# Residual rows kept in SBUF over four stages, zero fills moved, three stages rewritten as skewed pipelines

## The reference

```
h = relu(windowed product of x with filt * W_k + b_k)      # token:      [64, 248, 64]
h = h + attention(layernorm(h))                            # attention:  8 heads of 8, patch and position scores mixed
h = h + ffn(layernorm(h))                                  # feed-forward: only the 123 rows of largest router score,
                                                           #   gelu(x w1 + b1) w2 + b2, times the score
h = h + recurrent(layernorm(h))                            # key, table, recurrent: q, k, v and gates, then a
                                                           #   sequential update of two small MLPs over 248 steps
h = h + experts(layernorm(h))                              # 8 experts, two of them chosen a row
```

## Time and profile before

| | us |
|---|---|
| median of three runs | 10781.3 (10769.8 to 10793.7) |
| profiled execution, span from first to last instruction (its own time) | 10794.5 |
| TensorE busy | 9005.6 (83%) |
| VectorE busy | 4911.9 (46%) |
| ScalarE busy | 2097.8 (19%) |
| GpSimd busy | 227.2 (2%) |

### The profile page before, as it was taken

One profiled execution on the slowest core, in us unless ns is written; L12 is line 12 of the kernel. 1 busy time (PEld: TensorE's weight loads), 2 busy tenths in 40 slices (PEclk: granted clock), 3 DMA queues, 4 the chain that ended last, 5 costly groups with the idle time before them and its releaser, 6 DMA issues. The chain is left out here.

```text
span 10794.5 us, 373142 instructions
## 1 busy us (share of the span) xinstructions
PE 9005.6 (83%) x152370; PEld 5786.4 (54%) x152370; DVE 4911.9 (46%) x13031; ACT 2097.8 (19%) x4839; POOL 227.2 (2%) x184
## 2 busy tenths in 40 slices
PE   6799953424699999999999999999999999967777
PEld 2466631122466676666666766667667666642222
DVE  3444435446634444444344444443443444445555
ACT  0233321221111111111111111111111111113343
POOL 0000000001100000000000000000000000000000
PEclk8799975557899999999999999999999999988888
DMA  2000001425311121211111211222222222200000
GB/s 61 8 11 11 11 22 39 137 41 105 85 30 55 54 57 53 56 55 55 56 55 52 57 54 56 79 74 82 69 75 81 73 76 77 61 19 12 12 9 11
DMA packets 961796, 563.30 MB, mean 52 GB/s; under 512 B 376334, under 2 KB 956694, under 8 KB 959766
## 3 DMA queue, kind: packets, MB, share of 16 engines
q1 hardware_dynamic: 947990, 544.62, 18.7%
q0 software_dynamic: 13312, 12.57, 0.6%
HBM read 331.63 MB, written 188.08 MB: 48 GB/s over the span
## 5 line engine op out<-in xcount | busy, mean ns | idle before, releaser
L2387 PE MATMUL bank<-mv,hdiag 128*32 128x144 f32 x63744 | 2052.5, 286 | 11.2 <-DVE hdiag L2580 9.5
L2387 PEld LDWEIGHTS bank<-mv,hdiag 128*32 128x32 f32 x63744 | 1933.5, 110 | 85.8 <-DVE hdiag L2580 12.5
L2440 PE MATMUL bank<-mvt,ydiag 128*32 128x256 f32 x31872 | 1942.6, 381 | 0.0
L2440 PEld LDWEIGHTS bank<-mvt,ydiag 128*32 128x32 f32 x31872 | 1038.1, 110 | 568.8 <-issue 1.0
L2289 PE MATMUL bank<-yth,r_ident 128*128 128x512 f32 x896 | 507.9, 678 | 119.3 <-ACT mv L2232 58.8
L2243 ACT ACTIVATE work<-work 128x128 f32<-128x128 f32 x498 | 154.3, 310 | 2223.1 <-DVE work L2570 2223.1
L431 PE MATMUL att_bank<-att_qa,att_ka 32*124 32x248 f32 x2048 | 583.0, 411 | 0.5 <-DVE att_qa L645 0.5
L421 PE MATMUL att_bank<-att_ka,att_qn 32*124 32x496 f32 x1024 | 577.0, 661 | 3.7 <-DVE att_mx L606 3.7
L606 DVE TENSOR_REDUCE att_mx<-att_bank 124x2 f32<-124x496 f32 x512 | 344.9, 675 | 491.1 <-PE att_bank L421 491.1
L2613 DVE TENSOR_TENSOR rep<-bank,ta 128x128 f32<-128x128 f32 x249 | 72.7, 292 | 997.2 <-PE bank L2387 997.2
L2232 ACT ACTIVATE mv<-bank 128x256 f32<-128x256 f32 x1024 | 313.1, 388 | 836.6 <-PE bank L2321 836.5
(11 more groups left out here) (416 smaller groups left out, 11379.5 us busy)
## 6 DMA issues: line engine op xcount, KB each, us to landing
ring<-between_slopes SPq DMA_DIRECT2D x320, 512.0 KB, 4.1
baset<-between_base_old SPq DMA_DIRECT2D x265, 128.0 KB, 2.1
baset<-between_base SPq DMA_DIRECT2D x265, 128.0 KB, 2.2
between_base<-work SPq DMA_DIRECT2D x256, 128.0 KB
hist<-h SPq DMA_DIRECT2D x1992, 8.0 KB
hist<-y SPq DMA_DIRECT2D x1992, 2.0 KB
hist<-dl SPq DMA_DIRECT2D x1992, 8.0 KB
between_base_old<-bo SPq DMA_DIRECT2D x240, 128.0 KB
```

The source lines that it names most:

```text
L2387: mm = e.matmul(psP[32 * j:32 * j + 32, 0:MW], hdiag[:, hf, r, j, :], mv1[:, hf, r, j, :], start=(hf == 0 and r == 0), stop=(hf == 1 and r ...
L2440: mm = e.matmul(psBack[hf][32 * j:32 * j + 32, :], ydiag[:, n, j, :], both, start=(n == 0), stop=(n == 7))
```

## The change

- `HB` ([124, 64, 2, 64] float32, 32 KB a partition) is allocated once and holds h from the token stage to the end of the key stage. Token writes its rows there; attention adds to it in place; feed-forward reads it, adds norm and result in place and stores H2 from it, for the experts; key reads it. H0, H1 and XN are gone, and with them their stores and loads. X0 and H2 stay.
- Token: two buffers each for x and the norm; the first x is loaded before the weights, and each load stands two groups ahead of its use in SyncE's order.
- Attention: after its constants GpSimd sets a buffer `zero` (16 KB a partition) and issues the zero fills, 23 transfers, most of them contiguous with 16 KB a partition. The key stage's SyncE waits for them.
- Feed-forward normalisation: a pipeline skewed over four groups; the norm of all groups stays in `XB`. The square, the product with the router's weights and the sum of norm and rows are done by GpSimd.
- Main loop: `u`, `t2` and `gg` have eight buffers and the work is skewed by quarter groups; GpSimd squares; one VectorE instruction in place of two follows (the constant 0.044715 moves into tanh's scale); VectorE's order is uw(k-1), gg(k-3).
- Key: skewed over groups with two buffers of everything; GpSimd makes the norm's squares and the squares of q and k, ScalarE copies two of the gates; sequences of one half are neighbours, so a store moves pieces of 1 KB and 64 B.
- The loops of these stages are written out in full for all 16 groups. `Places` gives the semaphore value of each instruction's place in the written order.

```diff
 # token, SyncE
+                def load(n):
+                    if n >= 2:
+                        T.wait(e, n, "xt", 2)
+                    e.dma_start(xin[:, n % 2, :, :], ...).then_inc(xin_in[n % 2].sem, 16)
+                load(0)
 ...
+                load(1)
+                for n in range(G):
+                    if n + 2 < G:
+                        load(n + 2)
+                    store(n)
 # attention, VectorE
-                            hin.wait(e, t.n(-3), "h")
-                            out.count(e, t.n(-3))
-                            e.tensor_tensor(h1[:, :, :], bank[5][0:TL, 256:384].rearrange("p (a d) -> p a d", a=2), ht[:, :, :], ALU.add)
+                            h = HB[:, bass.ds(t.n(-3), 1), :, :].rearrange("p b a d -> p b (a d)")
+                            e.tensor_tensor(h, bank[5][0:TL, 256:384].unsqueeze(1), h, ALU.add)
 # feed-forward normalisation, GpSimd
+                for n in range(G + 4):
+                    if n < G:
+                        V.wait(e, "cen", n)
+                        if n >= 2:
+                            V.wait(e, "ssq", n - 2)
+                        e.tensor_tensor(sq[:, n % 2, :, :], rows(XB, n), rows(XB, n), ALU.mult)
+                    m = n - 3
+                    if 0 <= m < G:
+                        V.wait(e, "xn", m)
+                        if m >= 2:
+                            V.wait(e, "w", m - 2)
+                        e.tensor_tensor(xr[:, m % 2, :, :], rows(XB, m), wrb[:, :].unsqueeze(1).to_broadcast([TL, 8, D]), ALU.mult)
+                        e.tensor_tensor(rows(HB, m), rows(HB, m), rows(XB, m), ALU.add)
 # feed-forward main loop, GpSimd
+                for k in range(K):
+                    A.wait(e, "u", k)
+                    if k >= 8:
+                        V.wait(e, "gg", k - 8)
+                    e.tensor_tensor(t2[:, k % 8, :], u[:, k % 8, :], u[:, k % 8, :], ALU.mult)
 # and VectorE
+                    if 0 <= k - 1 < K:
+                        P.wait(e, "uu", k - 1)
+                        e.scalar_tensor_tensor(out=t2[:, b, :], in0=t2[:, b, :], scalar=1.0 / 0.044715, in1=u[:, b, :], op0=ALU.add, op1=ALU.mult)
+                    if 0 <= k - 3 < K:
+                        A.wait(e, "th", k - 3)
+                        e.scalar_tensor_tensor(out=gg[:, b, :], in0=t2[:, b, :], scalar=1.0, in1=u[:, b, :], op0=ALU.add, op1=ALU.mult)
 # key, order of VectorE's work in a turn n
+            v_order += [(q, n) for q in ("mean", "meand", "cen")] * (n < G)
+            v_order += [("xT", n - 2)] * (0 <= n - 2 < G)
+            v_order += [(q, n - 1) for q in ("ssq",)] * (0 <= n - 1 < G)
+            v_order += [(q, n - 2) for q in LATE] * (0 <= n - 2 < G)        # silu, four
+            v_order += [(q, n - 1) for q in ("rstd", "xn")] * (0 <= n - 1 < G)
+            v_order += [(q, n - 2) for q in ("g1", "g2", "ss", "mx", "rn", "kn")] * (0 <= n - 2 < G)
+            p_order += [("sq", n)] * (n < G) + [("k2", n - 2)] * (0 <= n - 2 < G)
+            a_order += [("xT", n - 2)] * (0 <= n - 2 < G) + [(f"sg{i}", n - 2) for i in range(4)] * (0 <= n - 2 < G)
+            a_order += [("std", n - 1)] * (0 <= n - 1 < G) + [(q, n - 2) for q in ("g0", "g3", "v", "nrm")] * (0 <= n - 2 < G)
 # key, SyncE
+                zeros(e)
+                for n in range(G):
 ...
+                            e.dma_start(dst[:, r0:r0 + 4, :].rearrange("t b d -> t (b d)"),
+                                        kqv[:, n % 2, w, 4 * a:4 * a + 4, :].rearrange("p b d -> p (b d)")).then_inc(out[n % 2], 16)
 # fills, GpSimd
+            def flat(t, first, n):
+                step = 128 * 64 * D
+                for at in range(first, first + n, step):
+                    k = min(step, first + n - at)
+                    fill(t[at:at + k].rearrange("(p f) -> p f", p=128), zero[:, 0:k // 128])
```

More of the change, by code:

```diff
@@ L203, in _ @@
                 e.preload_act_table(ACT.Sqrt)
-                def group(n, before):
+                for n in range(G):
                     T.wait(e, n, "xt")
@@ L837, in hidden @@
-                def hidden(n, half):
-                    for i in (2 * half, 2 * half + 1):
-                        q, a = i // 2, i % 2
-                        A.wait(e, n, f"u{i}", 1)
-                        e.matmul(bank[2 + i][:, 0:2 * L], w1s[:, 128 * a:128 * a + 128], xT[:, 2 * L * q:2 * L * q + 2 * L],
-                                 start=True, stop=True).then_inc(TS.sem, 1)
+                        mm = e.transpose(bank[k // 4][0:D, TL * (k % 4):TL * (k % 4) + TL], rows(XB, n)[:, k, :], ident[0:TL, 0:TL])
@@ L862, in _ @@
                 start(0)
-                hidden(0, 0)
-                hidden(0, 1)
-                with e.Fori(1, G) as n:
-                    start(n)
-                    hidden(n, 0)
-                    output(n - 1)
-                    hidden(n, 1)
-                    turn(n - 1)
-                output(G - 1)
-                turn(G - 1)
+                for n in range(G + 2):
+                    if n < G:
+                        hidden(n, 0)
+                        hidden(n, 1)
+                    if 0 <= n - 2:
+                        turn(n - 2)
+                    if n < G:
+                        hidden(n, 2)
+                        hidden(n, 3)
+                    if n + 1 < G:
+                        start(n + 1)
+                    if 0 <= n - 1 < G:
+                        output(n - 1)
@@ new lines, in key_layer, with stored @@
+        for n in range(G):
+            t_order += [("xT", n)] + [(f"f{i}", n) for i in range(4)]
+        V, A = Places(S.sem("vector"), v_order), Places(S.sem("scalar"), a_order)
+        P, T = Places(S.sem("pool"), p_order), Places(S.sem("tensor"), t_order)
+        out = [S.sem(f"out{q}") for q in range(2)]
+        def stored(e, n):
+            e.wait_ge(out[n % 2], 16 * 8 * (n // 2 + 1))
+        rows = lambda n: HB[:, 4 * n:4 * n + 4, :, :].rearrange("p b a d -> p (b a) d")
+        spread = lambda t: t.unsqueeze(2).to_broadcast([TL, 8, D])
@@ L1063, in _ @@
+                for n in (G - 2, G - 1):
+                    stored(e, n)
             @block.tensor
@@ L1112, in _ @@
             @block.vector
             def _(e):
-                e.memset(zero[:, :], 0.0).then_inc(s_v, 1)
                 e.memset(eps[:, :], EPS).then_inc(s_v, 1)
```

665 lines of the change are left out of this document (327 added, 338 removed).

## The result

| | before | after |
|---|---|---|
| median of four runs each, us | 10787.5 (10769.8 to 10797.1) | 10154.6 (10127.8 to 10169.6) |
| ratio, 95% interval | | 0.9414 (0.9396 to 0.9433) |
| profiled span, us | 10794.5 | 10144.3 |
| TensorE / VectorE busy, us | 9005.6 / 4911.9 | 8906.6 / 4818.3 |
| ScalarE / GpSimd busy, us | 2097.8 / 227.2 | 2091.6 / 410.1 |

The account below looks back on a forecast made before the run. TensorE was taken to bound attention; token, normalisation, main loop and key each had limits of their own. Savings 108 + 132 + 67 + 251 = 558 us off the 10794.5 span, less 13, gave 10223 us (10125 to 10350).

Parts of the forecast that it names:

- Token: Token stage: loading x ahead into two buffers cuts the period from 16.46 to 9.0 us; saves 108 us.
- Attention: Attention turns: TensorE stays the bound, 21 MB of fills hidden in 62 us; saves 0, unchanged within 5 us.
- GpSimd beside VectorE: Feed-forward and key loops: GpSimd's instructions and VectorE's with two SBUF inputs take turns; 1.18 us for 512 elements, 2.1 for 1024.
- Normalisation: Feed-forward normalisation: no transfers, 5.3 us a group, 100 us in all; saves 132 us (109 to 152).
- Main loop: Feed-forward main loop: 12.0 us a group with turns and eight handovers, 213 us in all; saves 67 us.
- Key: Key stage: a chain of 15.4 us a group with stores hidden, 262 us in all; saves 251 us.
- A: Rival: GpSimd runs free beside VectorE in main loop, normalisation and key; 10132 us, chance 0.14.
- B: Rival: TensorE stays at half clock in token as well, so less is saved there and in main loop; 10338 us, chance 0.08.
- C: Rival: key-stage stores stay a bound, 21.4 us a group by bytes, 90 us more; 10313 us, chance 0.16.
- E: Rival: the zero fills on GpSimd's queue last into the key stage, 62 us if none hidden; 10285 us, chance 0.04.
- D: Rival: written-out loops of token, feed-forward and key wait for code, 12 us a group; slower at 10991 us, chance 0.02.
- The 13 us taken off the span: Whole kernel: the runs' median lies 13 us below the profiled span, so 10236 became 10223.

Follow-up runs that it names:

- before_two_x: The kernel before with two x buffers in its token stage, each load issued a group ahead; token stage 209.5 us, run 10717.6 us.
- write_only: The changed kernel with GpSimd's normalisation and main-loop instructions replaced by memsets that read nothing from SBUF; normalisation 65.1 us, main loop 175.0, run 10128.3.
- combined: The changed kernel with paced fills, squares of main loop, normalisation and key on ScalarE, and VectorE reordered; run 10129.2 us, ratio 0.9407 to the kernel before.
- key_pieces: The changed kernel with key-stage stores in pieces of 256 B (gates 16 B), 3968 a group instead of 992; key 308.9 us, run 10227.9.

## Why the prediction was right, and where it was off

- **Token** (108; measured 112.1): right by its steps. Period 8.68 for 9.0, clock 0.98. `before_two_x` adds what the sum had not separated: 46 of it need more than the second x buffer, rows that are not stored and a second norm buffer; which of the two wasn't tested.
- **Attention** (0; measured -5.7): the step that failed is the fills' size, 21 MB for 29.7, and so their cover. The price, 11 us of waiting (16 with the clock of the first turns), lies within the stated 62. It looked small because one stretch at half clock fewer and the missing last store stood against it. "Unchanged within 5 us" missed by 0.7.
- **GpSimd beside VectorE**: the mechanism is shown by `write_only`: turns between GpSimd's reads and VectorE's second input. The size of each delay is near the taken one (1.23 for 0.69 in key).
- **Normalisation** (132; measured 150.9): mis-sized in two terms. The period was taken as 5.3 and is 4.77, since GpSimd's square takes 1.04 for 1.18 and the reductions fill the gaps between turns; and the 15 us for start and skew are 5 (81.3 - 16 x 4.77). The "free" end of the range, 80 us, was wrong as an end: `write_only` takes 65.
- **Main loop** (67; measured 85.7): the period was taken as 12.0 and is 10.9 in the mean, nearly all of the 19 us; filling and draining are 20 for 21 (194.4 - 16 x 10.9). The eight handovers and TensorE's "12.3 until its clock has risen" were too dear: the clock came to 0.77 for 0.57.
- **Key** (251; measured 260.2): the chain is the forecast one link by link; period 14.64 for 15.4 (GpSimd's 1024 squares 1.89 for 2.1, less idle between links). Stores are hidden, as taken. The fills' move and the pieces are worth 39 and 56 us of it.
- **Rivals.** A's number, 10132, is nearer to 10155 than the forecast, but not its mechanism: the interference is worth some 31 us of these two loops. B: the clock in token is 0.98. C: no release by a store in key. E: the fills ended at 253.7 us. D, code brought in late, did not make the written-out loops slow: token's period has no idle time but 0.35. Its mechanism exists, though, in a loop that is not written out, and cost 22 us in `combined`.
- **What no step had**: the recurrent stage's 46 us, 18 of TensorE's clock and 28 of its wait for `mv`. The tensors' places in memory are excluded. Some of the 46 is only which executions were profiled: the two spans are 34 us further apart than the medians of all spans. At least 13 us separate the stage's two groups of profiles, and their cause stays open. A place of VectorE's code like that in the table stage shows in 19.4 us of idle time of the kernel before, but no row ties TensorE's wait to it.
- **The numbers.** All four savings came out larger than in the sum, so 10223 for 10155 is no balance of large errors; the 616 us between the medians of the spans are 58 above the 558. Two steps of the arithmetic were wrong. The 13 us taken off the span are no constant: the changed kernel's profiled execution took 10146.1 us for a span of 10144.3, so the 13 were the distance of one execution from the median. And the low end put 262, the key stage's time, where its saving of 251 belongs; it would be 10136, still below the measured time.

The terms add up (token, attention, normalisation, main loop, key, recurrent, the rest): 558 + 4.1 - 5.7 + 18.9 + 18.7 + 9.2 + 46.0 + 1.0 = 650.2, the difference of the spans.

## What to carry to other kernels

Before handing an elementwise instruction to GpSimd, look for ScalarE's idle time: in this main loop ScalarE's squares brought all of what they took over, GpSimd's a part of it. Place VectorE's reductions where GpSimd reads, not its two-input instructions or small scalings. Size a burst of background transfers in bytes and pace it, and after every edit compare the stages that it didn't touch: a new idle time called "issue" there may be a price of the edit. Before a difference in an untouched stage is ascribed to the edit, take several profiles of either kernel.

## What the runs showed of the hardware that was not expected

- TensorE's granted clock falls to 0.50 for some 14 us while TensorE is busy without a gap; each stretch costs 6.3 us in attention, and profiles of one code differ by several (attention 1231.0 and 1237.1, recurrent 6760.3 and 6776.9 in two profiles of the changed kernel).
- A scaling of 124 x 8 elements on VectorE took 1.15 us for 0.17 beside GpSimd's reading instruction, and 0.27 in the mean beside a writing one.
- A loop's code may have to be brought in again on its passes, depending on the number of instructions ahead of it: 16 more or fewer on VectorE made 22 us in a stage of 230.
- 3968 pieces of 256 and 16 B take about 17 us when two groups may be under way, with SyncE issuing 98% of the time and the transfer engines busy for 32% (`key_pieces`); 992 of 1 KB and 64 B are hidden in 14.6.
- With 29.7 MB of fills under way, a norm load of 62 KB was used 20.9 us after its issue, and 9.4 us after it with the fills paced.
